# A filler matmul of 32-bit weights instead of a bf16 mask, ahead of each head's scores in turns without expert blocks

## The reference

```
xn = layernorm(x); x = x + attention_l(xn) + feed_forward_l(xn)
```

## Time and profile before

| | |
|---|---|
| runs | 2113.86, 2115.21, 2119.34 us (median 2115.21) |
| the profiled execution | 2109.61 us, span 2107.8 us |
| mean granted clock of TensorE | 0.863 |
| TensorE matmul busy | 1658.5 us (79%), 12743 |
| VectorE busy | 1242.1 us (59%) |
| ScalarE busy | 772.9 us (37%) |
| GpSimd busy | 381.8 us (18%) |

### The profile page before, as it was taken

The page is one execution under the profiler, slowest core; times in us unless marked ns, Lnnn a source line. Parts: engine busy times, 40 slices in busy tenths (PEclk is TensorE's granted clock), DMA queues, the critical chain, the costliest instruction groups (busy, mean ns, idle before and its releaser), DMA issues.

```text
span 2107.8 us, 44050 instructions
## 1 busy us (share of the span) xinstructions
PE 1658.5 (79%) x12743; PEld 1058.8 (50%) x12743; DVE 1242.1 (59%) x3512; ACT 772.9 (37%) x1723; POOL 381.8 (18%) x488
## 2 busy tenths in 40 slices
PE   3276799999766769899886388888883598888888
PEld 3122466766322558778776135555541245454544
DVE  6544455556665476556656356666662666666664
ACT  2022344444322423223222045555551224444444
POOL 1264210101444111111112600000015200000000
PEclk9866799999877778889886579999995679999999
DMA  7021465665211000000000223333321011111110
GB/s 229 29 71 43 132 205 178 188 192 156 57 44 48 0 1 1 0 0 0 0 1 1 72 81 114 119 122 115 110 85 34 18 36 42 44 43 42 40 44 14
DMA packets 133291, 145.07 MB, mean 69 GB/s; under 512 B 15001, under 2 KB 114130, under 8 KB 132946
## 3 DMA queue, kind: packets, MB, share of 16 engines
q1 hardware_dynamic: 100946, 106.20, 16.5%
q10 hardware_dynamic: 26112, 25.17, 4.0%
q0 software_dynamic: 6144, 12.60, 2.0%
HBM read 104.65 MB, written 39.52 MB: 68 GB/s over the span
## 4 chain that ended last, share of the span: by engine, by line
PE 52%; DVE 22%; issue 13%; another core or an unknown queue 4%; DMA 3%; ACT 2%; DVEq 1%; POOL 1%; SPq 1%; ACTq 0%; POOLq 0%
PE pO L706 7%; PE pH L594 5%; PE pT_ L567 5%; PE pY L602 5%; DVE X L1303 4%; PE pH L504 4%; DVE mx L1264 3%; PE pS L653 3%; PE pS L675 3%; DVE stk L1270 2%; PE pT_ L494 2%; PE pT_ L565 2%; PE pY L516 2%; PE pT_ L556 1%
## 5 line engine op out<-in xcount | busy, mean ns | idle before, releaser
L816 ACT ACTIVATE pex<-pT_ 128x512 f32<-128x512 f32 (+1 forms) x768 | 427.8, 562 | 665.0 <-PE pT_ L567 260.3
L1264 DVE TENSOR_REDUCE mx<-pS 128x2 f32<-128x512 f32 x512 | 346.6, 688 | 212.4 <-PE pS L544 86.6
L567 PE MATMUL pT_<-stk 32*128 32x256 f16 x1024 | 205.5, 290 | 83.1 <-DVE mx L1264 46.2
L544 PE MATMUL pS<-stk 32*128 32x256 f16 x1024 | 215.5, 299 | 34.3 <-DMA stk<-packed_qk 19.2
L706 PE MATMUL pO<-pex,va 128*9 128x256 f32 (+1 forms) x3072 | 206.9, 391 | 2.0 <-ACT pex L816 2.0
L809 ACT ACTIVATE wb<-pH,b 128x256 f32<-128x256 f32 x256 | 107.3, 470 | 271.0 <-PE pH L504 271.0
L906 POOL TENSOR_TENSOR qk<-qkf,qk 128x512 f16<-128x512 f32 x48 | 55.5, 1156 | 732.5 <-DVE qk L1240 367.0
L567 PEld LDWEIGHTS pT_<-stk 32*128 32x128 f16 x1024 | 55.6, 94 | 212.3 <-DVE mx L1264 94.3
L504 PE MATMUL pH<-XT,w 128*128 (+1 forms) x512 | 146.1, 412 | 0.0
L819 ACT ACTIVATE xts<-pO 128x256 f32<-128x256 f32 x192 | 73.9, 385 | 175.2 <-PE pO L706 126.1
L594 PE MATMUL pH<-xsT,wb 128*128 128x128 f32 x888 | 131.4, 293 | 1.8 <-ACT hbs L787 1.8
(11 more groups left out here) (197 smaller groups left out, 2903.2 us busy)
## 6 DMA issues: line engine op xcount, KB each, us to landing
wb<-in_w SPq DMA_DIRECT2D x111, 514.0 KB, 3.8
stk<-packed_qk ACTq DMA_DIRECT2D x96, 256.0 KB, 2.6
packed_qk<-qk SPq DMA_DIRECT2D x144, 128.0 KB, 1.9
xsb<-sorted_x SPq DMA_DIRECT2D x111, 64.0 KB, 3.4
sorted_y<-ysb SPq DMA_DIRECT2D x111, 64.0 KB, 3.1
sorted_x<-wb SPq DMA_DIRECT2D x3, 1536.0 KB, 12.5
w<-in_w SPq DMA_DIRECT2D x2, 1024.0 KB
out<-X SPq DMA_DIRECT2D x16, 128.0 KB, 1.8
```

The costliest lines, as they stand in the source:

```text
L544: return pe.matmul(bank[:, part * T:(part + 1) * T], stk[rows, side, j, part * P:(part + 1) * P], stk[rows, side, j, T:2 * T], start=True, ...
L567: return pe.matmul(bank[:, part * T:(part + 1) * T], key, stk[rows, side, j, 0:T], start=True, stop=True)
L816: act.activation(pex[:, k % 8, 0:n], bank[:, 0:n], ACT.Exp).then_inc(s("T_free"), 1)
L1264: ins = dve.tensor_reduce(mx[:, :, j, col], bank.rearrange("p (c n) -> p c n", c=2), AX.X, ALU.max)
```

## The change

The filler reads other operands. Before, it multiplies the bf16 identity (weights) with one bf16 mask matrix repeated four times, 512 columns, in both layers. After, it multiplies 32-bit weights: in layer 0 matrix 4 of `wq0` as the weights and matrices 0 to 3 as 512 columns, in layer 2 matrix 2 of `wq2` and matrices 0 and 1 as 256 columns, into the first half of the bank. Number, place and waits of the fillers are as before.

```
             def keep_clock(turn, bank):

                 if turn.layer in SORTED and blocks_of(turn.layer, turn.n)[1] == 0:
-                    pe.matmul(bank.rearrange("p (c n) -> p c n", c=4), identb[:, :],
-                              maskb[:, 1, None, :].to_broadcast([P, 4, P]), start=True, stop=True)
+                    w, n = {0: (wq0, 4), 2: (wq2, 2)}[turn.layer]
+                    pe.matmul(bank[:, 0:n * P], w[:, n, :], w[:, 0:n, :], start=True, stop=True)
```

## The result

The change makes the kernel slower: 2154.54 us (median of 4, 2153.07 to 2155.10) against 2116.26 (median of 4, 2113.86 to 2119.34), ratio 1.0179 with a 95% interval of 1.0161 to 1.0197. The forecast was 2156. The profiled execution took 2153.07 us, its span is 2151.2, 43.4 above that of before.

What follows compares the result with a forecast made beforehand. No single engine bounds layer 0's block-free turns: TensorE's matmuls in line with VectorE's reductions, plus pauses. 108 - 44 - 27 + 4 = +41 us on 2109.6 gives 2151; with 5.6 for the median, 2156, range 2135 to 2178 (0.46).

Steps and rivals of the forecast that it cites:

- part 1: Block-free turns: each longer filler adds 0.64 us at full clock, 1.28 at half in layer 0; 0.215 and 0.43 in layer 2.
- parts 2 and 4: Layer 0: 41 fillers at half clock, 87 at full, growth 108 us; 20 of 41 heads go to full, giving back 27.
- part 3: Layer 0: of the 108 us growth, 44 us lie beside waits and are hidden, 64 are left.
- (a): Idle time in front of the key scores (L567), 40 us, takes in half of itself, 20 us of growth.
- (b): Five turns stop ScalarE for the packed rows; five fillers between projection and stop, 3.2 us each turn, hide 13 us.
- (c): After turn 2 TensorE waits 6.4 us for sorted tokens; the eight fillers after the second projection vanish there: 5 us.
- (d): Behind each projection and value step TensorE waits 0.4 and 0.6 us for VectorE: six turns, 6 us hidden.
- part 5: Layer 2, 256-column fillers: turn 0 about +2, turn 14 +2, turn 15 +1; sum +4 us, bounds -5 and +13.
- the fast rival: Layer 0: fillers queued behind the pauses run inside them, swallowing half of 44 us: -11 us, 2104; chance 0.11.
- no recovery: The clock does not recover in the half-clock stretches, layer 2 costs 8: +72 us, 2187 (2178 to 2205); chance 0.22.
- full recovery: Block-free turns run at full clock but for the pauses: +11 us, 2126 (2121 to 2135); chance 0.07.
- More is exposed: Waits at packing, sorted tokens and projections hide nothing and weight loads cost 0.1 us each: above 2205; chance 0.06.

Runs made afterwards that it cites:

- e1: The kernel before with no filler at all in the block-free turns (176 matmuls less): ratio to before 1.0094 (1.0070 to 1.0117).
- f1: The changed kernel, unedited, run again on a faster chip without the pauses: ratio to before 1.0198 (1.0149 to 1.0248).
- g2: The kernel before with the 32-bit filler in layer 0's turn 15 alone, bf16 elsewhere, on a chip with pauses: ratio to before 1.0058 (1.0034 to 1.0081).
- f0: The kernel before, unedited, run again on a faster chip without the pauses: 0.9986 (0.9960 to 1.0013) of 2001.26 us.
- g4: The kernel before without a filler in turn 15 of both layers, on a chip with pauses: ratio to before 0.9998 (0.9975 to 1.0022).
- g1: The kernel before with its bf16 filler cut from 512 to 256 columns, on a chip with pauses: ratio to before 1.0008 (0.9982 to 1.0035).
- e4: The changed kernel with one weight column in the filler instead of 128: ratio to before 1.0183 (1.0122 to 1.0245).

## Why the prediction was right, point by point

- **The price of a filler (part 1).** The array time is right, the load was put too low. 1.06 us to the scores instead of 0.32 is +0.74 in a back-to-back pair, 0.1 more than the prediction's 0.64: the first load does show there, which the prediction kept for the upper end only. Between fillers it is +0.74 too (1.38 against 0.64). Behind a 32-bit projection it was +0.64 (0.95 against 0.31), so there the load hides. At half clock 2.01 against 0.54, +1.47 where the prediction had 1.28.
- **How many at half clock, and what the clock gives back (parts 2 and 4).** Right in kind and size. Of 41 fillers at half clock 17 are left (34 of the 256 records have the half-clock length), and the busy time gives nearly the same: (59.22 + 95.35 - 128 x 1.11) / 0.97 = 13, some more partly. The prediction let 20 of 41 go; 24 went. The clock of turn 12 is 0.91 and of turn 14 0.78, just outside the 0.8 to 0.9 that was said. e1 shows the mechanism from the other side (0.56, 0.62 without filler) and f1 its end (0.98, 0.97).
- **What lies beside waits (part 3).** Right where it can be read: (a) idle time before L567 fell from 40.0 to 4.5 + 16.6 = 21.1 us (20 expected). (b) ScalarE's stops fell from 4.8, 2.9 and some 2.2 us to 1.2 once and 0.8 three times. (c) The first block is 10.8 us later (247.58 against 236.81), and so is GpSimd's work behind the second projection (228.93 against 218.18): the eight fillers after it cost nothing. (d) The waits at the projections (3.6 us and 0.4) are gone; with those at the value steps the prediction had 6. Turn 15 had nothing to hide behind, +10.4 us, shown alone by g2.
- **Layer 2 (part 5).** The sum was near by luck, its parts were not. Between first and last exponential turn 15 went from 15.3 to 19.3 us, and 3.4 us of it are left at layer 3's first exponential, not 1: on the first chip VectorE's combination did not take it in. Only where GpSimd's gathers end last (f0, f1) does the growth vanish. Turn 14 took 3.4 us more in place of 2, turn 0 1.1. Layer 3, which has no filler, took 4.5 us less (393.1 for 397.6), and that made up for it in the total. No run shows it to be the change's doing: on the chip of f0 and f1 the kernel before takes 393.1 there too, the changed one 394.1.
- **The pauses.** The prediction took them for a property of this kernel that no filler reaches. They are one of the chip or the moment. On the chain they grew, 21.2% of 129.6 and 15.7% of 198.4 us are 58.6 us against 44.1, so the growth was not swallowed by them, as the fast rival needed; without them the change costs the same 2%. The prediction kept them constant, so these 14.5 us are in the measured growth and in no term of the sum. Whether the longer filler lengthens them is not shown.
- **The sum for layer 0.** Array time of the fillers 87 x 0.215 + 41 x 0.43 = 36 us before, 111 x 0.86 + 17 x 1.71 = 124 after, +88. Back from the clock on other work 24 x 0.7 = 17, more on pauses 14.5. The stretches show +41.7 (111.0 to 122.3, 151.7 to 171.7, 15.9 to 26.3), so 44 us are left over for the waits, and the prediction had 44. This is what a balance of estimates leaves, without the exposed loads; measured of it are the 19 us of (a) and what (b) to (d) show. The prediction's own sum for layer 0 was +37. So the mechanism held, and that the forecast came within 2 us of the result is partly luck: layer 0 cost 5 us more, layer 2's three turns 4 more, and layer 3 gave 4.5 back.

The rivals: no recovery is refuted by the clock, full recovery (+11) by f1, where the clock recovers and the cost stays at 2%. "More is exposed" is refuted by the time; of what it said the loads did show, 0.1 us each behind score and output matmuls. The full-recovery rival underrated how little is left to hide growth in once TensorE is busy 97% of the time (90.05 of 92.60 us).

## What to carry to other kernels

A filler that holds the clock is worth its array time only as long as the other work gains more by it. Here none at all cost 0.9%, the old one (0.215 us of array time a head) was not beaten, half of it could not be told from it, twice as much cost 0.5% and four times 2%. Count its array time first; type and width changed it by one weight load of at most 0.1 us. Where no wait stands beside it a long one shows whole (10 us in turn 15), and leaving it out there cost nothing that could be told (g4). Price it at full clock by the nearest matmul in the trace, take off the idle time directly behind it and the waits of other engines that start before it, and value the clock by the other work that ran at half speed.

## What was not expected of the hardware

- The same kernel takes 2116 us on some chips (the first and that of g1 to g4) and 1997 to 2001 on two others. Of that 64 us lie in the seven turns (262.7 against 198.9), 24 of them in TensorE's same matmuls, at a lower clock, and 40 in one turn of layer 2 (57.6 against 18.0). The rest is mostly waits of up to 27 us for results of TensorE whose matmuls are recorded as long finished, practically all of them while GpSimd issues indirect DMAs. What delays them stays open; the other chips issue the same DMAs (192) and show none.
- A matmul with one weight column holds the clock as well as one with 128 (0.98 and 0.97 of full in the seven turns, e4), and removing the bf16 filler lets it fall to 0.56 and 0.62 (e1).
- One 32-bit matmul of 512 columns takes as long as four of bf16 behind a projection (0.95 and 0.96 us to the next line), and 0.1 us longer behind the score matmuls (1.05 against 0.97).
